# Mixture-of-experts kernel on one core: list entries of 32 bytes, logits in columns, pads from row buffers, and the adds' waits on the synchronising engine

## What is computed

```python
x = x + wkv(w, u, layernorm(x), ctx)            # decaying sums over time, by feature; y = numerator / denominator
xn = layernorm(x)
logits = xn @ gate_w.T                          # 8 experts
probs = softmax(logits); weights, chosen = top_k(probs, 2)
expert_out = (silu(xn @ gate[e].T) * (xn @ up[e].T)) @ down[e].T      # e: 2 of 8 experts a token, 256 wide
shared = sigmoid(xn @ shared_gate.T) * ((silu(xn @ sg.T) * (xn @ su.T)) @ sd.T)   # 1024 wide
out = x + sum(weights * expert_out) + shared
```

## Time and profile before

| | us |
|---|---|
| median of 3 runs | 589.91 |
| lowest and highest | 588.55, 594.93 |
| the profiled execution | 594.29 |
| its span | 592.4 |
| busy: TensorE, VectorE, GpSimd, ScalarE | 499.7, 424.5, 334.8, 276.9 |

### The profile page before, as it was taken

One profiled execution on the slowest core, in us unless ns is written; L12 is line 12 of the kernel. 1 busy time (PEld: TensorE's weight loads), 2 busy tenths in 40 slices (PEclk: granted clock), 3 DMA queues, 4 the chain that ended last, 5 costly groups with the idle time before them and its releaser, 6 DMA issues.

```text
span 592.4 us, 10167 instructions
## 1 busy us (share of the span) xinstructions
PE 499.7 (84%) x2703; PEld 266.4 (45%) x2703; DVE 424.5 (72%) x986; ACT 276.9 (47%) x534; POOL 334.8 (57%) x421
## 2 busy tenths in 40 slices
PE   1025899899989999999999976899999999999950
PEld 1012355455545555555554543455545555555520
DVE  4398896989888899898998875366656556555530
ACT  4639847484754765847645431333323233323210
POOL 5185956848657478486684450425364655555342
PEclk9999889999989999999999989799999999999995
DMA  8941105224544142132110400315566666766552
GB/s 313 394 172 32 37 18 178 37 71 143 45 82 161 38 148 83 55 143 72 55 35 24 143 18 20 91 35 105 97 109 104 116 108 108 132 111 115 92 71 36
DMA packets 25896, 58.42 MB, mean 99 GB/s; under 512 B 6308, under 2 KB 6450, under 8 KB 24306
## 3 DMA queue, kind: packets, MB, share of 16 engines
q0 software_dynamic: 9792, 20.65, 20.2%
q1 hardware_dynamic: 16050, 37.13, 19.7%
HBM read 37.69 MB, written 20.08 MB: 98 GB/s over the span
## 4 chain that ended last, share of the span: by engine, by line
PE 37%; DMA 17%; issue 13%; DVE 11%; POOL 7%; ACT 7%; POOLq 6%; SPq 1%; DVEq 0%; ACTq 0%
PE GU L878 21%; DMA out<-wall,idsa 11%; PE DN L893 10%; POOLq L575 5%; DMA xb<-x 4%; ACT wall L700 2%; PE HT L823 2%; PE XT L823 2%; DVE st L1076 2%; DMA out<-xb 1%; DVE wall L1066 1%; POOL out L579 1%; DVE hb L1192 1%; DVE th L1189 1%; POOL lists L469 1%
## 5 line engine op out<-in xcount | busy, mean ns | idle before, releaser
L878 PE MATMUL GU<-wall,xt 128*128 128x512 f16 x768 | 192.2, 392 | 4.4 <-DVE wall L1170 4.4
L893 PE MATMUL DN<-wall,hx 128*128 128x512 f16 (+1 forms) x618 | 153.1, 384 | 9.0 <-DVE hx L1197 5.2
L878 PEld LDWEIGHTS GU<-wall,xt 128*128 128x128 f16 x768 | 76.9, 102 | 75.9 <-issue 10.9
L579 POOL DMA_INDIRECT out<-wall,idsa x39 | 61.8, 1585 | 81.5 <-issue 41.5
L893 PEld LDWEIGHTS DN<-wall,hx 128*128 128x128 f16 x618 | 60.4, 99 | 85.3 <-DVE hx L1197 9.4
L657 ACT ACTIVATE hx<-HT 128x256 f16<-128x256 f32 x103 | 39.1, 380 | 125.8 <-PE HT L823 119.7
L1197 DVE TENSOR_TENSOR hx<-HT,hx 128x256 f16<-128x256 f32 x103 | 43.1, 419 | 64.8 <-ACT hx L657 49.5
L652 ACT ACTIVATE th<-GU,scl 128x256 f32<-128x256 f32 x103 | 48.6, 472 | 82.9 <-PE GU L878 80.0
L878 PE MATMUL GU<-wall,kb 128*128 x240 | 61.4, 379 | 0.2 <-DVE kb L1371 0.2
L1189 DVE SCALAR_TENSOR_TENSOR th<-th,GU 128x256 f32<-128x256 f32 x103 | 41.6, 404 | 24.7 <-ACT th L652 21.9
L878 PE MATMUL GU<-wall,xnb 128*128 x228 | 58.5, 379 | 0.2 <-DVE xnb L1371 0.2
(11 more groups left out here) (164 smaller groups left out, 756.4 us busy)
## 6 DMA issues: line engine op xcount, KB each, us to landing
wall<-wgu SPq DMA_DIRECT2D x12, 1024.0 KB, 9.0
wall<-wd SPq DMA_DIRECT2D x12, 512.0 KB, 10.6
xb<-x SPq DMA_DIRECT2D x16, 256.0 KB
cb<-ctx_t SPq DMA_DIRECT2D x16, 256.0 KB
xn_rows<-xnb SPq DMA_DIRECT2D x16, 256.0 KB
out<-xb SPq DMA_DIRECT2D x16, 256.0 KB
out<-yb SPq DMA_DIRECT2D x4, 256.0 KB
xb<-xn_rows,idsi POOLq DMA_INDIRECT x39
```

The costliest lines, as they stand in the source:

```text
L579: pool.indirect_dma_start(out, bass.IndirectOffsetOnAxis(ap=idsa[:, j:j + 1], axis=0), ye[j % RESULTS], None, compute_op=ALU.add).then_inc ...
L878: ins = nc.tensor.matmul(GU[par][:], lhs(xp, c), gate_up(base, wp, c), start=m == 0, stop=m == 3 * HC - 1)
L893: ins = nc.tensor.matmul(DN[:], hx[par][:, hp * IE + c * P:hp * IE + (c + 1) * P], down(base, wp, c), start=start and m == 0, stop=stop an ...
```

## The change

An entry of a list becomes eight equal numbers, 32 bytes; the lists' initial fill grows from 64 KB to 512 KB and a row of them from 512 to 4096 bytes. The copy after the read-back takes every eighth number. `ids_back` moves to the buffers `growth` and `decay`, now one tensor. ScalarE writes each tile's nine logits into their own columns of `lga`, VectorE's maximum writes its own columns of `mxa`, and the two copies and ScalarE's wait go; the softmax reads with a stride. The pads come from x buffers 3 and 4; x(2) is issued before them, x(3) waits for all of them, and the two waits on `ids_zst` of GpSimd and ScalarE go (the scatter's stays). The adds' waits go to SP, which after them counts up `may_add`, on which GpSimd waits alone. The diff's core:

```diff
-TOP_STEPS, GATE_STEPS, NORM_STEPS, SCALE_STEPS = 5, 1, 3, 10
+LW = 8
+TOP_STEPS, GATE_STEPS, NORM_STEPS, SCALE_STEPS = 3, 1, 3, 10
-        ids_dram = nc.dram_tensor("lists", ((LISTS + 1) * P, 1), I32).ap()
+        ids_dram = nc.dram_tensor("lists", ((LISTS + 1) * P, LW), I32).ap()
-        ids_back, ids_float = yb[0:NSLOT, 0:P].bitcast(I32), yb[0:NSLOT, P:2 * P]
+        ids_back, ids_float = by_time[0:NSLOT, 0:P * LW].bitcast(I32), yb[0:NSLOT, 0:P]
+        zeros, pad_rows = xb[:, 3 * XW:3 * XW + H], xb[:, 4 * XW:4 * XW + P * LW]
...
             def load_x(t):
                 wait_from(sp, out_st, (t - (NB - 1)) * 16)
                 wait_from(sp, x_ld, t * 16)
+                if t == 3:
+                    sp.wait_ge(ids_zst, ZEROS * 16)
                 sp.dma_start(xrow(t), rows(x, t)).then_inc(x_ld, 16)
...
+            load_x(2)
             sp.wait_ge(ids_zero, 2)
-            sp.dma_start(xn_dram[PADS:PADS + P, 0:H], yb[:]).then_inc(ids_zst, 16)
+            sp.dma_start(xn_dram[PADS:PADS + P, 0:H], zeros).then_inc(ids_zst, 16)
...
-            load_x(2)
-            sp.dma_start(ids_tiles[0:LISTS, :], xnb[:, 0:P].bitcast(I32)).then_inc(ids_zst, 16)
+            sp.dma_start(ids_tiles[0:LISTS, :], pad_rows.bitcast(I32)).then_inc(ids_zst, 16)
...
             store_sum(B - 1)
 
+            sp.wait_ge(waits_rdy, WAIT_STEPS)
+            for j in range(1, NSLOT):
+                for r in range(min(j, RESULTS)):
+                    if j < RESULTS:
+                        sp.wait_ge(added[r], 16)
+                    else:
+                        earlier = sp.value_load(before_i[0:1, r * NSLOT + j:r * NSLOT + j + 1],
+                                                min_val=16, max_val=16 * ((NSLOT + RESULTS - 1) // RESULTS))
+                        sp.wait_ge(added[r], earlier)
+                        plain(sp, earlier)
+                sp.sem_inc(may_add, 1)
...
-                pool.memset(yb[:], 0.0).then_inc(ids_zero, 1)
-                pool.iota(xnb[:, 0:P].bitcast(I32), [[1, P]], base=PADS, channel_multiplier=0).then_inc(ids_zero, 1)
+                pool.memset(zeros, 0.0).then_inc(ids_zero, 1)
+                pool.iota(pad_rows.bitcast(I32), [[1, P], [0, LW]], base=PADS, channel_multiplier=0).then_inc(ids_zero, 1)
...
-                if t == 0:
-                    pool.wait_ge(ids_zst, ZEROS * 16)
...
-                                            toki[:, t:t + 1], None).then_inc(scattered, 16)
+                                            toki[:, t * LW:(t + 1) * LW], None).then_inc(scattered, 16)
...
-                if j == RESULTS:
-                    pool.wait_ge(waits_rdy, WAIT_STEPS)
-                for r in range(min(j, RESULTS)):
...
+                wait_from(pool, may_add, j)
...
-                if isinstance(t, int) and t == 0:
-                    act.wait_ge(ids_zst, ZEROS * 16)
...
-                wait_from(act, top, t * TOP_STEPS)
-                nc.scalar.activation(lgt[:], LG[:, 0:RN], ACT.Copy, scale=scale(ROUTER, YINV)).then_inc(lg_rdy, 1)
+                nc.scalar.activation(lga[:, t * RN:(t + 1) * RN], LG[:, 0:RN], ACT.Copy, scale=scale(ROUTER, YINV)).then_inc(lg_rdy, 1)
...
-                if t is not None:
-                    TS(span(lga, t * E, E), lgt[:, 0:E], 1.0, None, ALU.mult).then_inc(top, 1)
-                    TS(span(mxa, t, 1), mx8[:, 0:1], 1.0, None, ALU.mult).then_inc(top, 1)
...
-            nc.vector.tensor_copy(ids_float, ids_back).then_inc(ids_f, 1)
+            nc.vector.tensor_copy(ids_float.unsqueeze(2), ids_back.rearrange("r (p a) -> r p a", a=LW)[:, :, 0:1]
+                                  ).then_inc(ids_f, 1)
```

More of the change, by code:

```diff
@@ L137, in build @@
         kb, yb, xnb = sb("kb", [P, H]), sb("yb", [P, H]), sb("xnb", [P, H])
-        growth, decay = sb("growth", [P, HC * T]), sb("decay", [P, HC * T])
+        by_time = sb("by_time", [P, 2 * HC * T])
+        growth, decay = by_time[:, 0:HC * T], by_time[:, HC * T:2 * HC * T]
         th = [sb(f"th{i}", [P, IE]) for i in range(2)]
@@ L150, in build @@
         scl = sb("scl", [P, (E + 2) * 5])
-        lgt, mx8, ix8 = sb("lgt", [P, RN]), sb("mx8", [P, 8]), sb("ix8", [P, 8], U32)
+        lga, mxa, ix8 = sb("lga", [P, B * RN]), sb("mxa", [P, B * 8]), sb("ix8", [P, 8], U32)
         sg = sb("sg", [P, 1])
-        lga, mxa, chosen = sb("lga", [P, B * E]), sb("mxa", [P, B]), sb("chosen", [P, TOPK])
+        chosen = sb("chosen", [P, TOPK])
         gate = sb("gate", [P, B])
@@ L157, in build @@
         posf = sb("posf", [P, TOPK])
-        posi, toki, listi = sb("posi", [P, B * TOPK], I32), sb("toki", [P, B], I32), sb("listi", [P, 1], I32)
+        posi, toki, listi = sb("posi", [P, B * TOPK], I32), sb("toki", [P, B * LW], I32), sb("listi", [P, 1], I32)
         eidi, idsi, wsl = sb("eidi", [P, NSLOT], I32), sb("idsi", [P, NSLOT], I32), sb("wsl", [P, NSLOT])
@@ L204, in build @@
             "sq sq_sum sq_red exponents scale_step w_hi w_ws w_lo")
-        masked, ranked, listed, scattered, probs_st, weighed, rt, rt_exp, rt_tiles, rt_pos, pads_rdy = sems(
-            "masked ranked listed scattered probs_st weighed rt rt_exp rt_tiles rt_pos pads_rdy")
+        masked, ranked, listed, scattered, probs_st, weighed, rt, rt_exp, rt_tiles, rt_pos, pads_rdy, may_add = sems(
+            "masked ranked listed scattered probs_st weighed rt rt_exp rt_tiles rt_pos pads_rdy may_add")
         ids_zero, ids_zst, ids_ld, ids_f, ids_t, ids_rdy = sems("ids_zero ids_zst ids_ld ids_f ids_t ids_rdy")
@@ L312, in _ @@
                     load_ctx(1)
+            load_x(2)
             sp.wait_ge(ids_zero, 2)
-            sp.dma_start(xn_dram[PADS:PADS + P, 0:H], yb[:]).then_inc(ids_zst, 16)
-            sp.dma_start(xn_dram[PADS:PADS + P, H:XW], yb[:, 0:E]).then_inc(ids_zst, 16)
+            sp.dma_start(xn_dram[PADS:PADS + P, 0:H], zeros).then_inc(ids_zst, 16)
+            sp.dma_start(xn_dram[PADS:PADS + P, H:XW], zeros[:, 0:E]).then_inc(ids_zst, 16)
             for r in range(RESULTS):
-                sp.dma_start(out[PADS + r * P:PADS + (r + 1) * P, :], yb[:]).then_inc(ids_zst, 16)
-            load_x(2)
-            sp.dma_start(ids_tiles[0:LISTS, :], xnb[:, 0:P].bitcast(I32)).then_inc(ids_zst, 16)
-            sp.dma_start(ids_tiles[LISTS:LISTS + 1, :], xnb[0:1, 0:P].bitcast(I32)).then_inc(ids_zst, 16)
+                sp.dma_start(out[PADS + r * P:PADS + (r + 1) * P, :], zeros).then_inc(ids_zst, 16)
+            sp.dma_start(ids_tiles[0:LISTS, :], pad_rows.bitcast(I32)).then_inc(ids_zst, 16)
+            sp.dma_start(ids_tiles[LISTS:LISTS + 1, :], pad_rows[0:1, :].bitcast(I32)).then_inc(ids_zst, 16)
             load_expert(0)
@@ L373, in other_consts @@
                                         base=0, pattern=[[1, P]], channel_multiplier=-1))
-                link(pool.iota(toki[:], [[P, B]], base=0, channel_multiplier=1))
+                link(pool.iota(toki[:], [[P, B], [0, LW]], base=0, channel_multiplier=1))
                 for buf, pattern, channel in ((iota8, [[1, E]], 0), (iotaj, [[1, NSLOT]], 0), (iotap, [[0, 1]], 1),
@@ L636, in router_out @@
                 act.wait_ge(logits, t + 1)
-                wait_from(act, top, t * TOP_STEPS)
-                nc.scalar.activation(lgt[:], LG[:, 0:RN], ACT.Copy, scale=scale(ROUTER, YINV)).then_inc(lg_rdy, 1)
+                nc.scalar.activation(lga[:, t * RN:(t + 1) * RN], LG[:, 0:RN], ACT.Copy, scale=scale(ROUTER, YINV)).then_inc(lg_rdy, 1)
                 act.wait_ge(lg_rdy, t + 1)
                 wait_from(act, gated, t * GATE_STEPS)
-                nc.scalar.activation(sg[:], lgt[:, E:E + 1], ACT.Tanh, scale=0.5).then_inc(gate_tanh, 1)
+                nc.scalar.activation(sg[:], lga[:, t * RN + E:(t + 1) * RN], ACT.Tanh, scale=0.5).then_inc(gate_tanh, 1)
             def probs_exp(k, first, last):
@@ L1105, in small_steps @@
                     dve.wait_ge(lg_rdy, t + 1)
-                    nc.vector.max(mx8[:], lgt[:, 0:E]).then_inc(top, 1)
+                    nc.vector.max(mxa[:, t * 8:(t + 1) * 8], lga[:, t * RN:t * RN + E]).then_inc(top, 1)
                 if k is not None:
@@ L1123, in small_steps @@
                     dve.wait_ge(top, t * TOP_STEPS + 1)
-                    nc.vector.max_index(ix8[:], mx8[:], lgt[:, 0:E]).then_inc(top, 1)
+                    nc.vector.max_index(ix8[:], mxa[:, t * 8:(t + 1) * 8], lga[:, t * RN:t * RN + E]).then_inc(top, 1)
                 if k is not None:
@@ L1304, in logits_off_max @@
                 step(TT(r_d[:, first * E:last * E].rearrange("p (t e) -> p t e", e=E),
-                        lga[:, first * E:last * E].rearrange("p (t e) -> p t e", e=E),
-                        mxa[:, first:last].unsqueeze(2).to_broadcast([P, n, E]), ALU.subtract))
+                        lga[:, first * RN:last * RN].rearrange("p (t e) -> p t e", e=RN)[:, :, 0:E],
+                        mxa[:, first * 8:last * 8].rearrange("p (t e) -> p t e", e=8)[:, :, 0:1].to_broadcast([P, n, E]),
+                        ALU.subtract))
```

## The result

The changed kernel takes **571.42 us** (median of 4 runs, 570.85 to 572.98). The kernel before, run beside it, has 591.96 us (4 runs with the three shown ahead, 588.55 to 594.93). The ratio is 0.9659, 95% interval 0.9594 to 0.9724. Forecast: 572, range 565 to 580. The profiled execution's span is 569.2 us where 570.4 was predicted.

The account below looks back on a forecast made before the run. Transfers at four places, not engines, were taken to set the time. Gains of 4.4 + 4.8 + 1.1 + 3.5 + 4.0 = 17.8 us from the 589.9 median gave 572 us; its own range 569 to 575, low end 565, high end 580.

Parts of the forecast that it names:

- Start, 4.4 us: Kernel start: issuing x(2) ahead of the pad stores brings it at 24.0 instead of 28.4; 4.4 us gained, bounds 3.4 and 6.1.
- rival 3: At the start, x(3) behind the pads takes x(2)'s place: 574 us, or 576.5 with all the gain lost; chance 0.12.
- Lists, 4.8 + 1.1 us: Before the lists' read-back: 32-byte entries drain without backlog, 4.8 us gained, and a shorter TensorE gap saves 1.1 of clock loss.
- rival 2: In the lists' writes, 32-byte entries drain as slowly as 4-byte ones: 5.9 us lost, 578 us; chance 0.14.
- the stall at 150 us: Late store and x load near 150 us: 4.2 us, taken as chance, counted in the profiled execution only.
- The 1.1 for the clock: After TensorE's gap before the lists: clock loss falls from 2.8 us to 1.7 to 1.8; 1.1 us gained.
- Logits, 0: Two small VectorE copies a tile go, beside a full TensorE: 0 gained, bounds 0 and 4.9.
- inherited the stall: The 4.23 us stall of a VectorE copy at 338.77, under GpSimd's subtractions, was expected to move to L1151.
- SP, 3.5 us of pace and 4.0 of tail: Experts' stage, adds' waits moved to SP: slots gain 3.5 us (bounds 0 and 4.7), the tail 4.0 (0 and 4.5).
- the first gap: TensorE's first wait in the experts' stage, about 1 us, expected to stay because adds 0 to 5 chain on landings.
- Rival 5: In the experts' stage, SP's loads are slow, steps above 1.13 us, and SP falls behind TensorE: 598 us; chance 0.04.

## Why the prediction was right, step by step

- **Start, 4.4 us: right.** x(2) was down at 24.11 (24.0 taken); TensorE's first product came 4.3 us earlier, and the order undone cost 4.4 (by the ratios 3.4). x(3) never waited, so rival 3 didn't arise; 36.58 against 36.5 foreseen.
- **Lists, 4.8 + 1.1 us: right for the trace, low for the time.** The gap is 2.37 us, 2.4 was predicted, and the clock fell to 1.2 GHz for 3.4 us instead of 10.2. The reason, how closely the entries lie, held in the experiments against the size of a write (rival 2); the block itself stays an inference. Undone it cost 7.8 (by the ratios 6.7), not 5.9: 0.9 of it is that the gap was 8.1 us there and not 7.2, and what was left out of the term is the stall at 150 us. The 1.1 for the clock is less sure than I had it (last section).
- **The stall at 150 us: a wrong step.** I called it chance and "absent from the median". Both profiled executions with 4-byte entries packed show it, in the same place (TensorE idle 2.5 and 3.0 us of 20), and none of the other twelve, where no gap of TensorE between 130 and 310 us is over 0.61 us. So it goes with the entries. Nor is it true that the other tiles' scatters did no harm. From the issue of an x store to the load that waits for its landing it takes 2.3 us in eight of the changed kernel's ten turns from 85 to 265 us, and 4.8 at most. With packed 4-byte entries it takes over 3 us in seven (before) and six (undone) of the ten, 8.8 and 8.4 us in the longest. Only the longest held up TensorE more than in the changed kernel. How often unprofiled runs have it isn't shown: three of the four runs of the undone kernel were 3 to 5 us below the profiled one. The median of before on which the sum stood, 589.91, rose to 591.96 with one more run, and was 592.77, 589.2 and 591.56 beside the experiments. By the medians the gain was 20.5, and not 17.8 (the ratio's interval is 16.3 to 24.0 us, so it holds both). That the forecast of 572 hit to 0.6 us is partly luck: a low median and a low sum cancelled.
- **Logits, 0: right**, and L1153 (L1151 before) inherited the stall, as named, at 331 (near 334 foreseen). Only my reason was loose: "two elements and a tensor_scalar". What the traces show is told in the last section.
- **SP, 3.5 us of pace and 4.0 of tail: the mechanism right, both terms low** (5.3 and 4.7 against the undone kernel, both beyond the bounds given, 4.7 and 4.5). GpSimd needs 3.19 us a slot, 3.2 was predicted. I had kept about 1 us of the 4.7 for the first gap, of which 0.73 stays, and nothing else does. In the tail add 36 starts 0.28 us after its rows, not 0.7; adds 37 and 38 come 8.06 and 10.6 us after them (8.2 and 10.8 foreseen).
- **Rival 5**: the bound is real and steeper than priced. SP's loads took 0.263 us (median), a step 0.63, 2.5 us of the 4.54 a slot has.

## To carry to other kernels

Give each element that a scatter writes 16 or 32 bytes of its own: the same 4-byte writes took 15.9 us side by side and 2.1 us at a distance of 32 bytes (2.4 at 16), and beside the backlog plain stores were late too, 8.8 us instead of 2.3 at worst. Waits and loads of wait values can go to an engine with an empty stream, if the steps of one slot fit well into the slot: 0.56 of it was safe, 1.2 times of it cost 58 us, and every change of expert added its landing on top. When an instruction is taken out from under a stall, look for the next one of its kind, and move what causes the stall instead.

## What the runs showed that I had not expected

**Which instructions a GpSimd subtraction holds up.** It is not the smallness. Line L1136 of the changed kernel is a multiplication of 16 elements, in every tile:

```profile
L1136 DVE TENSOR_TENSOR pos<-ones,pos x16: 160/168/1115, 91.1 to 343.4; 128x16 f32<-128x16 f32 x16
```

Five of the sixteen began under a long GpSimd multiplication and took 3.6 to 6.6 times as long. Additions that read a PSUM bank (L1126, L1135), and the scalar_tensor_tensor of L1102 and L1191, which read one too, kept their time in all such places (9, 9, 9 and 14 of them after 150 us). All that were held up (L1153, L1136, the two-element L1132 six times of ten, L1143 once, the scans L1061 and L1064 three times before 50 us, the copy of the earlier trace rows, L1307 above) have all their operands in SBUF; not all such are: the maximum and its index (L1111, L1129) and the reciprocals (L1078) beside them kept their time. Which starts first doesn't decide it by itself: L1307 began 0.2 us before the subtraction by its row (the instruction ahead of it ran until 0.12 us before) and still ended with it, while L1136 at 112.73, 0.02 us ahead of a multiplication, kept its 0.17 us. The Trainium skill (GPSIMD Engine Reference, Key points) says that GpSimd shares its SBUF interfaces with VectorE, against instructions with two SBUF inputs or in a two-port mode. L1136 and L1307 have two such inputs and agree with it; L1153, L1132 and the copy have one, and no row shows in which mode they ran.

**A short stand of TensorE doesn't always cost the clock.** After TensorE stood 7.22 us (before) or 8.11 us (4-byte entries), half clock lasted 10.2 us. After 2.3 to 2.4 us at the same place it lasted 3.4 us in eight of the twelve other profiled executions, and in four the clock stayed full, as in the one with the logits' copies:

```profile
356.00:366.00 10.00, 7.63 (x38) 3.51 (x36) 4.21 (x13) 3.98 (x7) 3.89 (x4) 1.00 0.30 84
```

After the stand of 3.05 to 3.2 us under the subtraction, half clock lasted 3.4 us in seven of eleven, 6.8 in one, and in three the clock stayed full. What decides it isn't shown. It is 1.7 us (10 us at 0.83), about the size of the differences between single runs of one kernel, and more than the 0.9 us that the logits' copies seemed to win.
